# Router logits computed with the router's weights stationary, turned by VectorE and placed by DMAs

## The chip, the cores and the metric

The kernel runs on one core of a Trainium2 chip. The metric is the device time of one execution in microseconds (us); a lower number is better. The engines of the core are named PE (TensorE's matmuls), PEld (TensorE's weight loads), DVE (VectorE), ACT (ScalarE), POOL (GpSimd) and SP (SyncE, which issues all of this kernel's DMAs; its queue is written SPq).

## The reference, cut to what matters

A batch of 8 images is cut into patches and embedded, joined with text tokens (548 tokens of 192 features per image), passed through one attention layer, and then through a mixture of experts. The change lies in the mixture of experts, and there in the first two lines only:

```python
logits = jnp.einsum('td,ed->te', xt, router_w)      # 4384 tokens, 192 features, 16 experts
probs = jax.nn.softmax(logits, axis=-1)
topk_w, topk_idx = jax.lax.top_k(probs, 8)
topk_w = topk_w / jnp.sum(topk_w, axis=-1, keepdims=True)
comb = zeros((T, 16)).at[arange(T)[:, None], topk_idx].add(topk_w)
for e in range(16):                                  # 8 experts of width 128, 8 of width 256
    h = gelu(xt @ w1[:, off:off + wd])
    out = out + comb[:, e:e + 1] * (h @ w2[off:off + wd, :])
```

## The kernel before

The first part of the program (until about 240 us) is the attention of the eight images. From there on the mixture of experts runs, over nine token tiles: t = 0 to 7 with 512 tokens each, t = 8 with 288. Each token tile takes 24 steps, k = 0 to 23, one for each 128 rows of the experts' hidden width. Tokens are columns: `x2` holds the normalised tokens with features on the partitions, and one step is a chain over four engines:

- `up` on PE: five matmuls into a PSUM bank (three banks in turn), 128 hidden rows by 512 tokens
- `gelu` on ACT (L884): PSUM to `act`
- `weigh` on DVE (L1303): `act` times `gate`, the expert's weights of all tokens, spread over the partitions
- `act_round` on ACT (L674, tile `act_hi`), then `act_rest` on DVE (L1035, tile `act_lo`): the two parts of `act` that fp32r matmuls read
- `down` on PE: five matmuls that read `act_hi` and `act_lo` and add into the output's banks

PE runs ahead of itself: in its program `up(j + 3)` stands before `down(j)`, with j counting the steps of all tiles. DVE's loop runs, for each j, `weigh(j + 1)`, `act_rest(j)` and then the side work of step k (function `beside`); ACT's runs `gelu(j + 1)`, `act_round(j)`, side work. All `act` tiles exist three times, so `gelu(j)` waits for `act_rest(j - 3)` and `act_round(j)` for `down(j - 3)`.

The side work prepares the next tile, t + 1, while tile t runs. For the router of tiles 2 to 8 it is, before the change:

- PE, after `down` of step 11: `logits(t + 1)`. The tokens' columns are the weights, 128 at a time, and the router's 32 columns move (16 experts, with the rounded and the remaining part of their weights side by side). Four groups of 128 tokens times three matmuls make twelve; three groups of 96 make nine for t + 1 = 8. The result has tokens on partitions, in PSUM bank 3.
- DVE, step 13: `router_shift` (L1187 to L1191, tiles `lsum`, `lmax`, `lsub`) adds the two parts and takes off the maximum.
- ACT, step 13: `logits_exp` (L815, tile `lexp`). Exp and gelu need different tables, so a table load stands before it and another before the next gelu.
- DVE, steps 14 to 17: `router_top`, `router_left`, `router_weights` (tile `comb`) and `turn_comb` (L1227, tile `ct_t`), which turns the weights in 32x32 blocks.
- SP: `store_ct` (L371) writes `ct_t` to `comb_dram`, four DMAs that put the blocks in place; `gates` (L458) spreads one expert's row over the partitions of one of four `gate` buffers, one DMA per expert.

SP's program has a fixed order. In tile t, behind the gates of experts 10 to 13, it holds `store_out(t - 1)` (six DMAs, L463), `load_res(t + 2)` (L424), `load_rb(t)` (six DMAs, L405), the gates of experts 14 and 15 and `store_ct(t + 1)`. Expert 14 is first weighed in step 20, expert 15 in step 22, and expert 0 of the next tile in the `weigh` that stands in step 23.

Of the kernel before, what the change touches and what calls it, by code (L numbers as in the profile page):

```python
# [32 lines left out]
P = 128  # L33
# [23 lines left out]
E = 16  # L57
# [28 lines left out]
def width(t):  # L86
    return WIDTHS[t]


def segs(t):  # L90

    return SEG if width(t) % (SEG * BLOCK) == 0 else SEG - 1
# [7 lines left out]
def ct_after(t):  # L100

    return 16 * sum(ct_dmas(u) for u in range(t + 1))
# [53 lines left out]
def early_fusion(nc, first_patches, patches, txt, tok_w, tok_b, gammas, gn_w, gn_b, attn_w, w1, w2, out):  # L156
# [3 lines left out]
    def sb(name, shape, dt=F32, scope=ctx):  # L160
        return scope.enter_context(nc.sbuf_tensor(name, shape, dt))

    def sem(name):
        return ctx.enter_context(nc.semaphore(name))

    with ctx:
# [67 lines left out]
        ot = [ot0, ot1]  # L234
        out_t = sb("out_t", [HD, TW])
        ct_t = sb("ct_t", [P, SEG * BLOCK])

        aw_hi, aw_lo = sb("aw_hi", [P, 2, AW], F32R), sb("aw_lo", [P, 2, AW], F32R)
        rw = sb("rw", [P, 2, 2, E], F32R)
# [64 lines left out]
        down_done, sums_read, out_ready = sem("down_done"), sem("sums_read"), sem("out_ready")  # L304
        out_stored, ld_rb = [sem(f"out_stored{i}") for i in range(2)], [sem(f"ld_rb{i}") for i in range(2)]
        xn2_turned, x2_stored, ld_x2, ct_turned = sem("xn2_turned"), sem("x2_stored"), [sem("ld_x2_0"), sem("ld_x2_1")], sem("ct_turned")
        h_stored, ld_res = sem("h_stored"), [sem(f"ld_res{i}") for i in range(3)]

        block = ctx.enter_context(nc.Block())
# [18 lines left out]
        def _(sp):  # L328
# [44 lines left out]
            def x2_rows(t):  # L373
                return x2_dram[0:D * width(t)].rearrange("(d n) -> d n", d=D)
# [10 lines left out]
            def load_x2(t):  # L385

                n = width(t)
                sp.wait_ge(x2_stored, 16 * sum(width(u) // segs(u) // BLOCK for u in range(BY_BLOCKS, t + 1)))
                sp.dma_start(x2_raw[:, 0, 0:n], x2_rows(t)[0:P, :]).then_inc(ld_x2[0], 16)
                for p0 in (0, HD):  # L390
                    sp.dma_start(x2_raw[p0:p0 + HD, 1, 0:n], x2_rows(t)[P:D, :]).then_inc(ld_x2[1], 16)

            def block_views(rows_, t):

# [53 lines left out]
            def gates(t, first, end):  # L448
                n = width(t)
                for e in range(first, end):  # L450

                    last = LAST_OF[(e - 4) % E] + 1
                    if e >= 4:
                        sp.wait_ge(gated, nth(t, NW, last))
                    elif t:
                        sp.wait_ge(gated, nth(t - 1, NW, last))
                    src = comb_dram[e, FROM[t]:FROM[t] + n].partition_broadcast(P)
                    sp.dma_start(gate[e % 4][:, 0:n], src).then_inc(ld_gate[e % 4], 16)  # L458

            def store_out(t):  # L460
                sp.wait_ge(out_ready, t + 1)
                for dst, src in block_views(out_rows, t):
                    sp.dma_start(dst, src).then_inc(out_stored[t % 2], 16)  # L463
# [22 lines left out]
            for t in range(1, NTT):  # L486
                nxt = t + 1 < NTT
                sp.wait_ge(ct_stored, ct_after(t))
                gates(t, 0, 8)
                if nxt:  # L490
                    store_x2(t + 1)
                gates(t, 8, 10)
                if nxt:
                    load_x2(t + 1)
                gates(t, 10, 14)
                store_out(t - 1)
                if t + 2 < NTT:
                    load_res(t + 2)
                load_rb(t)
                gates(t, 14, 16)  # L500
                if nxt:
                    store_ct(t + 1)
# [167 lines left out]
        def _(sc_eng):  # L670
# [250 lines left out]
            def beside(t, k):  # L921

                if t + 1 == NTT:
                    return
                if k == 0:
                    second_norm(t + 1, 0)
                elif k == 1:
                    second_norm(t + 1, 1)
                elif k == 9:
                    x2_round(t + 1, 0)  # L930
                elif k == 10:
                    x2_round(t + 1, 1)
                elif k == 13:
                    logits_exp(t + 1)

            gelu(0)
# [11 lines left out]
        def _(dve):  # L948
# [230 lines left out]
            def wide(ap):  # L1179
                return ap.unsqueeze(2).broadcast_to([ap.shape[0], ap.shape[1], E])  # L1180

            def router_shift(t, bank=U_BANK):
                n = segs(t)
                r = width(t) // n
                dve.wait_ge(lg_done, t + 1)
                parts = ps[:r, bank, 0:n * 2 * E].rearrange("p (g i e) -> p g e i", g=n, i=2)
                dve.tensor_reduce(lsum[:r, 0:n, :], parts, AX.X, ALU.add)  # L1187
                dve.drain()
                dve.tensor_reduce(lmax[:r, 0:n], lsum[:r, 0:n, :], AX.X, ALU.max)
                dve.drain()  # L1190
                dve.tensor_tensor(lsub[:r, 0:n, :], lsum[:r, 0:n, :], wide(lmax[:r, 0:n]), ALU.subtract).then_inc(l_sub, 1)  # L1191
# [175 lines left out]
            def beside(t, k):  # L1367

                if k in (4, 5, 6):
                    turn_out(t - 1, (k - 4,))  # L1370
                elif k in (7, 8):
                    add_out(t - 1, (k - 7,))
                elif k == 11:
                    add_out(t - 1, (2,))
                if 20 <= k < 23 and t + 2 < NTT:
                    second_part(t + 2, k - 20)
                if t + 1 == NTT:
                    return
                if k in (2, 3):
                    turn_x2(t + 1, k - 2)  # L1380
                elif k == 9:
                    x2_rest(t + 1, 0)
                elif k == 10:
                    x2_rest(t + 1, 1)
                elif k == 13:
                    router_shift(t + 1)
                elif k == 14:
                    router_top(t + 1)
                elif k == 15:
                    router_left(t + 1)  # L1390
                elif k == 16:
                    router_weights(t + 1)
                elif k == 17:
                    turn_comb(t + 1)

            weigh(0)
# [13 lines left out]
        def _(pe):  # L1410
# [200 lines left out]
            def logits(t, bank=U_BANK):  # L1611
                n = segs(t)
                r = width(t) // n
                pe.wait_ge(x2_lo, nth(t, 2, 2))
                if t == 0:
                    pe.wait_ge(rw_ready, 1)
                elif t == BY_BLOCKS:
                    pe.wait_ge(ct_copied, BY_BLOCKS)
                for g in range(n):
                    c = slice(g * r, (g + 1) * r)  # L1620
                    x = [x2[t % 2][:, i, c] for i in range(3)]
                    near, rest = [rw[:, i, :, :].rearrange("p i e -> p (i e)") for i in range(2)]
                    last = series(ps[:r, bank, 2 * E * g:2 * E * (g + 1)], [(x[0], near), (x[1], near), (x[2], rest)])
                last.then_inc(lg_done, 1)

# [211 lines left out]
```

## Time and profile before

| | us |
|---|---|
| median of three runs | 765.95 (765.46 to 766.73) |
| the profiled execution | 763.07 |
| its span, first to last instruction | 761.3 |
| PE busy in the span | 719.3 (94%) |
| DVE busy | 582.1 (76%) |
| ACT busy | 467.0 (61%) |
| POOL busy | 153.0 (20%) |
| mean granted clock of TensorE | 0.994 |

The profile is that of one execution. A start time is counted from the beginning of the span. A row that ends in "x12" groups twelve instructions that follow each other; its duration is that of the whole group. Matmuls overlap, so a matmul of 0.39 us may be followed by the next after 0.23 us: what a matmul costs is the distance between starts. The bracket at a row's end is the time the engine was idle before it and what it waited for.

### The profile page before, as it was taken

The numbers are of one execution on the slowest core, as the hardware profiler recorded it, in microseconds if no ns is written. First come the engines' busy times: TensorE is split into PE (matmuls) and PEld (weight loads), VectorE is DVE, ScalarE is ACT, GpSimd is POOL, SyncE is SP. The second block draws the span as 40 slices with busy tenths as digits, with TensorE's granted clock in tenths as the row PEclk, the third lists the DMA queues.
The fourth block names the chain that finished last, engine by engine and source line by source line (L and its number), as shares of the span: only waits on it lengthen the run. The fifth ranks groups of instructions, "written<-read, shape, count | busy, mean of one in ns | idle before, by whom it ended". The sixth has DMA issues, their size and how long they took to land.

```text
span 761.3 us, 13137 instructions
## 1 busy us (share of the span) xinstructions
PE 719.3 (94%) x4265; PEld 605.2 (79%) x4265; DVE 582.1 (76%) x1616; ACT 467.0 (61%) x1041; POOL 153.0 (20%) x254
## 2 busy tenths in 40 slices
PE   5988999999998799999999999999999999999996
PEld 4777878888986577788888888888888888888895
DVE  7888988998888686677777777767777777677675
ACT  3677778778777646456456456456456456456453
POOL 3062654753543870000000000000000000000000
PEclk9999999999999999999999999999999999999998
DMA  6700011011022651455256255255265255244242
GB/s 196 210 23 22 1 45 44 13 34 44 30 79 65 166 163 45 97 136 128 74 132 128 76 134 125 77 131 132 72 128 136 74 133 121 73 132 94 46 87 43
DMA packets 120564, 70.13 MB, mean 92 GB/s; under 512 B 82000, under 2 KB 100496, under 8 KB 120496
## 3 DMA queue, kind: packets, MB, share of 16 engines
q1 hardware_dynamic: 120496, 69.31, 36.6%
q8 instruction: 33, 0.54, 0.3%
q14 instruction: 35, 0.29, 0.1%
HBM read 58.65 MB, written 10.63 MB: 91 GB/s over the span
## 4 chain that ended last, share of the span: by engine, by line
PE 66%; DVE 21%; ACT 4%; issue 3%; DVEq 3%; DMA 2%; SPq 1%; POOL 0%; POOLq 0%
PE ps L1412 65%; DVE sc L1072 4%; DVE pr L1094 4%; ACT pr L754 2%; DVE nm L1079 2%; DVE k_lo L1035 1%; DVE st L989 1%; DVE gst L1100 1%; DVEq L1077 1%; DVE h L1138 1%; DMA pat<-patches 1%; ACT xa_hi L674 1%; DVE act L1303 1%; DMA gate<-comb_dram 1%; DVE q_lo L1035 1%
## 5 line engine op out<-in xcount | busy, mean ns | idle before, releaser
L884 ACT ACTIVATE act<-ps 128x512 f32<-128x512 f32 (+1 forms) x216 | 124.7, 578 | 205.4 <-PE ps L1412 205.3
L1303 DVE TENSOR_TENSOR act<-act,gate 128x512 f32<-128x512 f32 (+1 forms) x216 | 145.5, 673 | 126.5 <-ACT act L884 117.1
L1412 PE MATMUL ps<-x,w_hi 128*128 128x512 f32 (+1 forms) x648 | 215.2, 387 | 2.2 <-ACT act L884 2.2
L1412 PE MATMUL ps<-x,w_lo 128*128 128x512 f32 (+1 forms) x432 | 165.4, 383 | 0.0
L1035 DVE TENSOR_TENSOR act_lo<-act,act_hi 128x512 fp32r<-128x512 f32 (+1 forms) x216 | 146.1, 676 | 0.2
L1412 PEld LDWEIGHTS ps<-x,w_hi 128*128 128x128 f32 x648 | 120.5, 188 | 27.1 <-ACT act L884 2.7
L674 ACT ACTIVATE act_hi<-act 128x512 fp32r<-128x512 f32 (+1 forms) x216 | 130.2, 603 | 3.2 <-DVE act L1303 3.1
L1412 PEld LDWEIGHTS ps<-x,w_lo 128*128 128x128 f32 x432 | 81.3, 188 | 16.5
L1412 PE MATMUL ps<-act_hi,w_hi 128*128 128x512 f32 (+1 forms) x216 | 83.2, 385 | 3.3 <-DVE act_lo L1035 3.3
L535 POOL TENSOR_TENSOR rstdb<-vepsb,neg_half 128x4 f32<-128x4 f32 x9 | 9.1, 1010 | 379.8 <-DVE vepsb L1168 379.8
L1412 PE MATMUL ps<-act_lo,w_hi 128*128 128x512 f32 (+1 forms) x216 | 83.2, 385 | 0.0
L1412 PE MATMUL ps<-act_hi,w_lo 128*128 128x512 f32 (+1 forms) x216 | 83.2, 385 | 0.0
L1412 PE MATMUL ps<-act_lo,w_r 128*128 128x512 f32 (+1 forms) x216 | 82.4, 381 | 0.0
L1412 PE MATMUL ps<-act_hi,w_r 128*128 128x512 f32 (+1 forms) x216 | 81.4, 377 | 0.0
L754 ACT ACTIVATE pr<-sc,nm 128x580 f32<-128x580 f32 (+4 forms) x120 | 66.3, 555 | 13.2 <-DVE nm L1079 13.2
L1561 PE MATMUL ps<-ident,pr 128*128 128x128 f32 (+1 forms) x360 | 45.3, 277 | 15.0 <-DVE q_lo L1035 6.7
L674 ACT ACTIVATE pt<-ps 128x384 f32<-128x384 f32 (+3 forms) x120 | 46.4, 470 | 17.0 <-PE ps L1561 16.8
L1561 PEld LDWEIGHTS ps<-ident,pr 128*128 128x128 f32 (+1 forms) x360 | 39.1, 133 | 20.1 <-issue 7.4
L1412 PEld LDWEIGHTS ps<-act_hi,w_hi 128*128 128x128 f32 x216 | 40.5, 188 | 14.8 <-DVE act_lo L1035 5.6
L1072 DVE CUSTOM_DVE_ANT_0 sc<-ps,decay 128x548 f32<-128x548 f32 (+4 forms) x120 | 49.4, 453 | 1.6 <-PE ps L1412 1.5
L1412 PEld LDWEIGHTS ps<-act_hi,w_r 128*128 128x128 f32 x216 | 40.6, 188 | 9.0
L1412 PEld LDWEIGHTS ps<-act_lo,w_r 128*128 128x128 f32 x216 | 40.4, 187 | 9.0
(183 smaller groups left out, 1200.3 us busy)
## 6 DMA issues: line engine op xcount, KB each, us to landing
gate<-comb_dram SPq DMA_DIRECT2D x128, 256.0 KB, 3.6
w_raw<-w SPq DMA_DIRECT2D x16, 384.0 KB, 3.7
h_dram<-h SPq DMA_DIRECT2D x8, 384.0 KB
res<-h_dram SPq DMA_DIRECT2D x8, 384.0 KB, 3.9
rb<-h_dram SPq DMA_DIRECT2D x48, 64.0 KB, 2.5
out<-rb SPq DMA_DIRECT2D x48, 64.0 KB, 1.9
x_dram<-xn_t SPq DMA_DIRECT2D x24, 96.0 KB, 2.4
gate<-comb_dram SPq DMA_DIRECT2D x16, 144.0 KB, 3.2
```

The source lines that it names most:

```text
L535: pool.tensor_tensor(rs[:, :], ve[:, :], neg_half[:, 0:n], ALU.pow)
L674: return a.activation(dst, src, ACT.Copy)
L754: last = a.activation(pr[s][:r, cols], sc[s][:r, cols], ACT.Exp, bias=nm[s][:r, I:I + 1], accum_out=row_sum[s][:r, I:I + 1])
L884: a.activation(act[j % 3][:, 0:n], ps[:, up_bank(j), 0:n], ACT.Gelu_apprx_tanh).then_inc(gelu_done, 1)
L989: dve.bn_stats(s6[:rows(I), I, :], tokens(h, b, I))
L1035: return dve.tensor_tensor(dst, src, hi, ALU.subtract)
L1072: dve.tensor_tensor_reduce(out=sc[s][:r, OFF[I]:OFF[I] + n], in0=psf[:r, at:at + n], in1=decay[:r, hh, 0:n], scale=1.0 / 8, scalar=0.0 if ...
L1079: dve.tensor_scalar(nm[s][:, cols], mx[s][:, cols], -1.0, None, ALU.mult).then_inc(nm_ready, 1)
L1094: last = dve.tensor_scalar(t, t, inv_den[s][:rows(I), I:I + 1], None, ALU.mult)
L1303: dve.tensor_tensor(act[j % 3][:, 0:n], act[j % 3][:, 0:n], gate[e % 4][:, 0:n], ALU.mult).then_inc(gated, 1)
L1412: return pe.matmul(dst, w, x, start=start, stop=stop)
L1561: return pe.transpose(ps[:n, bank, at:at + P], pr[s][:, src:src + n], ident[:, :])
```

## The change

For the tiles 2 to 8 the matmul is swapped: the router's 32 columns are the weights, and all tokens of the tile move, three matmuls of 512 columns (288 for tile 8) in place of twelve (nine). The result now has the 32 router columns on partitions and tokens along the row. DVE's `turn_logits`, in step 12, turns it in 32x32 blocks from PSUM into `lg_t`; SP's `place_logits`, four DMAs (three for tile 8) of 32 x 4 x 32 elements, puts the blocks in place in `lg`, with tokens on partitions as before; `router_shift` reads `lg` and waits for these DMAs. `router_shift` and `logits_exp` stand in step 14 in place of 13, and the DVE steps behind them are each one later, `turn_comb` in 18. Tiles 0 and 1 are as before.

```diff
--- before.py
+++ after.py
@@ -234,6 +234,7 @@
         ot = [ot0, ot1]
         out_t = sb("out_t", [HD, TW])
         ct_t = sb("ct_t", [P, SEG * BLOCK])
+        lg_t, lg = sb("lg_t", [BLOCK, TW]), sb("lg", [P, SEG, BLOCK])
 
         aw_hi, aw_lo = sb("aw_hi", [P, 2, AW], F32R), sb("aw_lo", [P, 2, AW], F32R)
         rw = sb("rw", [P, 2, 2, E], F32R)
@@ -304,6 +305,7 @@
         down_done, sums_read, out_ready = sem("down_done"), sem("sums_read"), sem("out_ready")
         out_stored, ld_rb = [sem(f"out_stored{i}") for i in range(2)], [sem(f"ld_rb{i}") for i in range(2)]
         xn2_turned, x2_stored, ld_x2, ct_turned = sem("xn2_turned"), sem("x2_stored"), [sem("ld_x2_0"), sem("ld_x2_1")], sem("ct_turned")
+        lg_turned, lg_placed = sem("lg_turned"), sem("lg_placed")
         h_stored, ld_res = sem("h_stored"), [sem(f"ld_res{i}") for i in range(3)]
 
         block = ctx.enter_context(nc.Block())
@@ -389,6 +391,14 @@
                 sp.dma_start(x2_raw[:, 0, 0:n], x2_rows(t)[0:P, :]).then_inc(ld_x2[0], 16)
                 for p0 in (0, HD):
                     sp.dma_start(x2_raw[p0:p0 + HD, 1, 0:n], x2_rows(t)[P:D, :]).then_inc(ld_x2[1], 16)
+
+            def place_logits(t):
+
+                sp.wait_ge(lg_turned, t - BY_BLOCKS + 1)
+                n = width(t) // segs(t) // BLOCK
+                for i in range(n):
+                    src = lg_t[:, 0:width(t)].rearrange("c (g i e) -> c i g e", g=segs(t), e=BLOCK)[:, i, :, :]
+                    sp.dma_start(lg[i * BLOCK:(i + 1) * BLOCK, 0:segs(t), :], src).then_inc(lg_placed, 16)
 
             def block_views(rows_, t):
 
@@ -493,6 +503,8 @@
                 if nxt:
                     load_x2(t + 1)
                 gates(t, 10, 14)
+                if nxt:
+                    place_logits(t + 1)
                 store_out(t - 1)
                 if t + 2 < NTT:
                     load_res(t + 2)
@@ -930,7 +942,7 @@
                     x2_round(t + 1, 0)
                 elif k == 10:
                     x2_round(t + 1, 1)
-                elif k == 13:
+                elif k == 14:
                     logits_exp(t + 1)
 
             gelu(0)
@@ -1179,11 +1191,19 @@
             def wide(ap):
                 return ap.unsqueeze(2).broadcast_to([ap.shape[0], ap.shape[1], E])
 
+            def turn_logits(t):
+                dve.wait_ge(lg_done, t + 1)
+                dve.transpose(lg_t[:, 0:width(t)], ps[0:BLOCK, U_BANK, 0:width(t)]).then_inc(lg_turned, 1)
+
             def router_shift(t, bank=U_BANK):
                 n = segs(t)
                 r = width(t) // n
-                dve.wait_ge(lg_done, t + 1)
-                parts = ps[:r, bank, 0:n * 2 * E].rearrange("p (g i e) -> p g e i", g=n, i=2)
+                if t < BY_BLOCKS:
+                    dve.wait_ge(lg_done, t + 1)
+                    parts = ps[:r, bank, 0:n * 2 * E].rearrange("p (g i e) -> p g e i", g=n, i=2)
+                else:
+                    dve.wait_ge(lg_placed, ct_after(t) - ct_after(BY_BLOCKS - 1))
+                    parts = lg[:r, 0:n, :].rearrange("p g (i e) -> p g e i", i=2)
                 dve.tensor_reduce(lsum[:r, 0:n, :], parts, AX.X, ALU.add)
                 dve.drain()
                 dve.tensor_reduce(lmax[:r, 0:n], lsum[:r, 0:n, :], AX.X, ALU.max)
@@ -1382,15 +1402,17 @@
                     x2_rest(t + 1, 0)
                 elif k == 10:
                     x2_rest(t + 1, 1)
-                elif k == 13:
+                elif k == 12:
+                    turn_logits(t + 1)
+                elif k == 14:
                     router_shift(t + 1)
-                elif k == 14:
+                elif k == 15:
                     router_top(t + 1)
-                elif k == 15:
+                elif k == 16:
                     router_left(t + 1)
-                elif k == 16:
+                elif k == 17:
                     router_weights(t + 1)
-                elif k == 17:
+                elif k == 18:
                     turn_comb(t + 1)
 
             weigh(0)
@@ -1616,10 +1638,14 @@
                     pe.wait_ge(rw_ready, 1)
                 elif t == BY_BLOCKS:
                     pe.wait_ge(ct_copied, BY_BLOCKS)
+                near, rest = [rw[:, i, :, :].rearrange("p i e -> p (i e)") for i in range(2)]
+                if t >= BY_BLOCKS:
+                    x = [x2[t % 2][:, i, 0:width(t)] for i in range(3)]
+                    series(ps[0:2 * E, bank, 0:width(t)], [(near, x[0]), (near, x[1]), (rest, x[2])]).then_inc(lg_done, 1)
+                    return
                 for g in range(n):
                     c = slice(g * r, (g + 1) * r)
                     x = [x2[t % 2][:, i, c] for i in range(3)]
-                    near, rest = [rw[:, i, :, :].rearrange("p i e -> p (i e)") for i in range(2)]
                     last = series(ps[:r, bank, 2 * E * g:2 * E * (g + 1)], [(x[0], near), (x[1], near), (x[2], rest)])
                 last.then_inc(lg_done, 1)
 
```

PE, at the end of step 11 of tile 2: `act_hi2` and `act_lo2` belong to `down` of step 11, `rw` is the router's weights, `x2_1` the tokens of tile 3; the row with `act_hi0` opens `down` of step 12. Before:

```order
L1412 MATMUL ps<-act_lo2,w2_r 128x512
L1412 MATMUL ps<-rw,x2_1 128x32 [waits x2_lo]
L1412 MATMUL ps<-rw,x2_1 128x32 x11
L1412 MATMUL ps<-x2_0,w1_hi 128x512 [waits gelu_done]
L1412 MATMUL ps<-x2_0,w1_lo 128x512
L1412 MATMUL ps<-x2_0,w1_hi 128x512 x2
L1412 MATMUL ps<-x2_0,w1_lo 128x512
L1412 MATMUL ps<-act_hi0,w2_hi 128x512 [waits act_lo_ready]
```

The same place after:

```order
L1434 MATMUL ps<-act_lo2,w2_r 128x512
L1434 MATMUL ps<-x2_1,rw 32x512 [waits x2_lo]
L1434 MATMUL ps<-x2_1,rw 32x512 x2
L1434 MATMUL ps<-x2_0,w1_hi 128x512 [waits gelu_done]
L1434 MATMUL ps<-x2_0,w1_lo 128x512
L1434 MATMUL ps<-x2_0,w1_hi 128x512 x2
L1434 MATMUL ps<-x2_0,w1_lo 128x512
L1434 MATMUL ps<-act_hi0,w2_hi 128x512 [waits act_lo_ready]
```

Twelve narrow matmuls became three wide ones at the same place.

DVE, steps 12 to 15 of a middle tile: `act0` to `act2` are the three buffers of `act`, and the row with `gate3` and `act2` is `weigh` of step 14. Before:

```order
L1035 TENSOR_TENSOR act_lo0<-act0,act_hi0 128x512 [waits act_hi_ready]
L1303 TENSOR_TENSOR act2<-act2,gate3 128x512 [waits ld_gate3,gelu_done]
L1035 TENSOR_TENSOR act_lo1<-act1,act_hi1 128x512 [waits act_hi_ready]
L1187 TENSOR_REDUCE lsum<-ps 128x64 [waits lg_done]
L1189 TENSOR_REDUCE lmax<-lsum 128x4
L1191 TENSOR_TENSOR lsub<-lsum,lmax 128x64
L1303 TENSOR_TENSOR act0<-act0,gate3 128x512 [waits ld_gate3,gelu_done]
L1035 TENSOR_TENSOR act_lo2<-act2,act_hi2 128x512 [waits act_hi_ready]
L1200 MAX top<-lexp 128x8 [waits l_exp]
```

The same place after:

```order
L1047 TENSOR_TENSOR act_lo0<-act0,act_hi0 128x512 [waits act_hi_ready]
L1196 STREAM_TRANSPOSE lg_t<-ps 32x512 [waits lg_done]
L1323 TENSOR_TENSOR act2<-act2,gate3 128x512 [waits ld_gate3,gelu_done]
L1047 TENSOR_TENSOR act_lo1<-act1,act_hi1 128x512 [waits act_hi_ready]
L1323 TENSOR_TENSOR act0<-act0,gate3 128x512 [waits ld_gate3,gelu_done]
L1047 TENSOR_TENSOR act_lo2<-act2,act_hi2 128x512 [waits act_hi_ready]
L1207 TENSOR_REDUCE lsum<-lg 128x64 [waits lg_placed]
L1209 TENSOR_REDUCE lmax<-lsum 128x4
L1211 TENSOR_TENSOR lsub<-lsum,lmax 128x64
L1323 TENSOR_TENSOR act1<-act1,gate0 128x512 [waits ld_gate0,gelu_done]
L1047 TENSOR_TENSOR act_lo0<-act0,act_hi0 128x512 [waits act_hi_ready]
L1220 MAX top<-lexp 128x8 [waits l_exp]
```

The wait for PE's logits stands one step earlier, and the shift is one step later behind a wait for the DMAs.

SP, behind the last gates of the first fourteen experts: `lg` is the placed logits, `rb0` the output rows, `res0` and `rb1` loads for later. After the change:

```order
L468 DMA gate1<-comb_dram 128x512 [waits gated]
L401 DMA lg<-lg_t 32x4x32 [waits lg_turned]
L401 DMA lg<-lg_t 32x4x32 x3
L473 DMA out<-rb0 32x16x32 [waits out_ready]
L473 DMA out<-rb0 32x16x32 x5
L434 DMA res0<-h_dram 128x4x192 [waits ln2_normed]
L415 DMA rb1<-h_dram 32x16x32 x6
L468 DMA gate2<-comb_dram 128x512 [waits gated]
L468 DMA gate3<-comb_dram 128x512 [waits gated]
L373 DMA comb_dram<-ct_t 16x4x32 [waits ct_turned]
```

The two rows on `lg` are new; before, the store of `out` followed directly on the gate.

## Rows read from the trace of the kernel before

**Rows 1.** Window 411.5 to 468.5 us (one token tile): busy us and instructions by engine, clock.

```profile
411.50:468.50 57.00, 57.00 (x254) 46.38 (x253) 41.53 (x91) 32.40 (x58) 1.79 (x3) 1.00 0.48 112
```

**Rows 2.** All waits of PE from 290 us to the end: total, times, longest.

```profile
PE ps L1412 <- DVE act_lo L1035: 1.1, 1, 1.1
```

**Rows 3.** Timeline of PE around the logits of tile 3: start, duration, instruction.

```profile
411.37 0.39 PE L1412 MATMUL ps<-act_lo,w_r 128*128 128x512 f32 x1
411.60 1.41 PE L1412 MATMUL ps<-rw,x 128*128 128x32 f32 x12
412.85 0.48 PE L1412 MATMUL ps<-x,w_hi 128*128 128x512 f32 x1
...
414.11 0.39 PE L1412 MATMUL ps<-act_hi,w_hi 128*128 128x512 f32 x1
...
418.75 0.39 PE L1412 MATMUL ps<-act_hi,w_hi 128*128 128x512 f32 x1
...
421.06 0.39 PE L1412 MATMUL ps<-act_hi,w_hi 128*128 128x512 f32 x1
```

**Rows 4.** Timeline of PE around the logits of tile 8 (288 tokens).

```profile
696.70 0.86 PE L1412 MATMUL ps<-rw,x 128*96 128x32 f32 x9
...
697.73 0.39 PE L1412 MATMUL ps<-x,w_lo 128*128 128x512 f32 x1
```

**Rows 5.** Timeline of DVE over the same stretch as rows 3.

```profile
411.27 0.69 DVE L1303 TENSOR_TENSOR act<-act,gate 128x512 f32<-128x512 f32 x1 [1.02 <-ACT act L884]
411.88 0.69 DVE L1035 TENSOR_TENSOR act_lo<-act,act_hi 128x512 fp32r<-128x512 f32 x1
413.04 0.29 DVE L1187 TENSOR_REDUCE lsum<-ps 128x64 f32<-128x128 f32 x1 [0.47 <-PE ps L1412]
...
416.16 0.69 DVE L1303 TENSOR_TENSOR act<-act,gate 128x512 f32<-128x512 f32 x1 [2.23 <-ACT act L884]
416.76 0.69 DVE L1035 TENSOR_TENSOR act_lo<-act,act_hi 128x512 fp32r<-128x512 f32 x1
```

**Rows 6.** Transposes on DVE from PSUM: duration min/median/max in ns.

```profile
L1320 DVE STREAM_TRANSPOSE out_t<-ps x9: 485/718/719, 339.3 to 754.9; 64x512 f32<-64x512 f32 x8, 64x288 f32<-64x288 f32 x1
```

**Rows 7.** Timeline of SP's queue over the same stretch.

```profile
408.74 3.03 SPq L463 DMA_DIRECT2D out<-rb  x6
...
415.88 1.33 SPq L458 DMA_DIRECT2D gate<-comb_dram  x2
423.62 1.73 SPq L371 DMA_DIRECT2D comb_dram<-ct_t  x4
```

**Rows 8.** DMAs issued from 395 to 456 us: KB each, median us to landing.

```profile
out<-rb SPq DMA_DIRECT2D x6, 64.0 KB, 1.9
...
rb<-h_dram SPq DMA_DIRECT2D x6, 64.0 KB, 2.7
x_dram<-xn_t SPq DMA_DIRECT2D x4, 96.0 KB, 2.4
...
comb_dram<-ct_t SPq DMA_DIRECT2D x4, 8.0 KB, 1.5
```

**Rows 9.** Timeline of ACT over the same stretch.

```profile
413.96 0.26 ACT L815 ACTIVATE lexp<-lsub 128x64 f32<-128x64 f32 x1 [0.90 <-DVE lsub L1191]
414.23 1.28 ACT L884 ACT_TABLE_LOAD   x1
415.53 0.60 ACT L884 ACTIVATE act<-ps 128x512 f32<-128x512 f32 x1
```

**Rows 10.** Timeline in tile 0: PE waits for a late `act_lo`.

```profile
284.85 0.69 DVE L1035 TENSOR_TENSOR act_lo<-act,act_hi 128x512 fp32r<-128x512 f32 x1
...
285.59 0.50 PE L1412 MATMUL ps<-act_hi,w_hi 128*128 128x512 f32 x1 [0.28 <-DVE act_lo L1035]
```

**Rows 11.** Gate loads issued at 415.8 to 416.3 us, landing.

```profile
gate<-comb_dram SPq DMA_DIRECT2D x1, 256.0 KB, 3.8
```

**Rows 12.** Gate loads issued at 509.9 to 510.5 us, behind the loads of `x_raw`.

```profile
gate<-comb_dram SPq DMA_DIRECT2D x1, 256.0 KB, 7.0
```

## The prediction

> **What bounds the kernel now.** I began with the busy time by stage, since the change touches only the router of tiles 2 to 8. In one token tile of the mixture of experts PE is busy for 57.00 of 57.00 us at full granted clock, DVE for 41.5 and ACT for 32.4 [rows 1]. Then the waits: from 290 us on PE waits once, for 1.1 us [rows 2]. So PE's instruction stream is the time of this stage. What leaves PE's stream is won in full, until one of PE's inputs is late; what goes onto DVE or a DMA costs nothing, until it makes `act_lo` late for `down`. Last I read the timelines of PE, DVE, ACT and SP around one set of logits. Ahead lie 6 tiles with 512 tokens (2 to 7) and one with 288 (8).
>
> **What PE saves.** `down` opens every (421.06 - 414.11) / 3 = 2.317 us, ten matmuls, so 0.232 us each [rows 3]. From the first logits matmul to the next `down` are 2.51 us, of which five matmuls of `up` are 1.16: the twelve cost 1.35 us [rows 3]. The new three move 512 columns each, as `up` and `down` do, so 3 x 0.232 = 0.70. Saved: 0.65 per tile. Tile 8: 697.73 - 696.70 - 0.23 = 0.80 for nine [rows 4]; three with 288 columns are 3 x 0.232 x 288/512 = 0.39 (an estimate by columns); saved 0.41. Sum: 6 x 0.65 + 0.41 = 4.3 us. That is the most the change can give, since nothing else leaves PE.
>
> **The wait in step 12.** DVE's `turn_logits` now waits for the logits one step earlier. In the times of tile 2: PE starts the third matmul at 411.60 + 0.46 = 412.06 and, with 0.39 us for it [rows 3], is done at 412.45. DVE starts at 412.48. A turn of 512 columns from PSUM takes 0.72 us [rows 6], on fewer partitions no less, so I take 0.71: done at 413.19. Behind it on DVE are `weigh` of step 14, which ran at 411.27 and now ends at 413.9, and `act_lo` of step 13, which ran at 411.88 [rows 5] and now ends at 414.5. `down` of step 13 opens at 414.11 - 0.65 + 2.32 = 415.78 [rows 3]. The delay of nearly 2 us and the extra 0.71 us of DVE are hidden by that lead: cost 0. ACT's next `act_round` gets its input at 413.9, about when the gelu before it is over.
>
> **The wait in step 14.** SP's queue is free (its last gate of that part goes out before the store at 408.74), so it issues at 413.2. The nearest DMA in form is the store of `ct_t`: four in 1.73 us, 0.43 apart [rows 7]. The fourth goes out at 414.5 and lands L later, so `router_shift` starts at 414.55 + L. DVE is through with the two steps ahead of it by 415.8. From there the old rows give the distances. Exp on ACT starts 413.96 - 413.04 = 0.92 after the shift's first instruction [rows 5, 9]. Behind exp come a table load of 1.28 and the gelu [rows 9], then `weigh`, `act_round` and `act_lo`, which ends at 416.76 + 0.69 = 417.45, 3.49 after exp began [rows 5]. Before, that `act_lo` was for `down` of step 14, opening at 418.75: 1.30 us of slack [rows 3]. After, it is for `down` of step 15, whose turn would come at 421.06 - 0.65 = 420.41. It is ready at 414.55 + L + 0.92 + 3.49 = 418.96 + L. A PE that waits restarts 0.05 us after `act_lo` ends, and its first matmul lasts 0.50 instead of 0.39, the weight load being no longer hidden [rows 10]: 0.16 together. So the stall is S = 418.96 + L + 0.16 - 420.41 = L - 1.3, if positive. One tile gains 0.65 - S = 1.95 - L.
>
> **L decides, and no row shows it.** No DMA in this trace goes from SBUF to SBUF. This one has 128 runs of 128 bytes, the store of `ct_t` 64 and lands in 1.5; the stores of `rb` have 512 and land in 1.9, those of `xn_t` 768 in 2.4 [rows 8]. Between the first two by runs: 1.5 + 0.4 x 64/448 = 1.56. A load from DRAM takes 2.7 with 512 runs [rows 8]; that one has to read DRAM, which this one need not, so 2.7 is the far end. The near end is 1.3, where S is zero; below that nothing more is won. I take 1.55, by the store of the same shape.
>
> The Trainium skill ("DMA: Bandwidth & Descriptors", the two cost components) gives a DMA a fixed cost of about 2.0 us, most of it the receipt of the write at the target. By that, L would be 2.0 and the gain gone. The stores of `ct_t` with 1.5 us speak against it here [rows 8]; whether an SBUF target does the same no row shows.
>
> **Sum.** S = 0.25, so 0.40 per tile: 6 x 0.40 = 2.4. Tile 8 has one DMA fewer (0.43) and a turn shorter by 0.23 [rows 6], against a slot that moves only 0.41 ahead in place of 0.65: its `act_lo` is on time and its 0.41 stay. Together 2.8 us. The profiled execution took 763.07 (a span of 761.3 and 1.8 around it) and would take 760.3; the median of the runs is 2.9 above that execution, so 765.95 - 2.8 = 763.2.
>
> **What SP pushes back.** The four DMAs hold the queue from 413.2 to 415.0. The store of `out`, the loads of `res` and `rb`, which took 415.88 - 408.74 = 7.14 us [rows 7], move from 408.74 to 415.0, and the gate of expert 14 from 415.88 to 422.1. It lands 3.8 later [rows 11], at 425.9. Its `weigh` in step 20 stands six steps behind that of step 14: 411.27 + 6 x 2.317 + 1.35 = 426.5 before, 426.1 after. Just in time; and late by up to 2.3 us would still cost nothing, since in a plain step `act_lo` ends about 2.5 us ahead of its `down` (412.57 against 416.43, less the 1.35 of logits [rows 3, 5]) and PE wants it some 0.2 early. `store_ct` moves with `turn_comb`: a step of 2.3 less the 0.4 saved, plus the 1.3 by which DVE's chain has come closer to PE, 3.1 us, from 423.62 to 426.7 [rows 7]. The first gate of the next tile then lands near 433.4, for a `weigh` at 435.4. Cost 0, with 2 us left. `load_res` and `load_rb` are used a good step or a whole tile later.
>
> **Rivals.**
> - No stall (L at 1.3 or less, or the chain behind exp a little shorter): the full 4.3 us, 761.7. For it: writes into SBUF may be acknowledged sooner than the stores to DRAM. Against it: twice the runs of `ct_t`. 0.22.
> - The stall eats the gain (L between 1.76 and 2.2). At L = 2.0: 6 x -0.05 + 0.41 = 0.1 us, 765.9. For it: the stores of `rb` at 1.9 and `xn_t` at 2.4 [rows 8]. This is where the skill's 2.0 leads. 0.25.
> - Slower by the same wait: each tile loses from L = 1.95, the whole from 2.02, by over 0.2% from 2.27. With the 2.7 of `rb` [rows 8]: 6 x 0.75 - 0.41 = 4.1 us more, 770.0. Against it: its source is DRAM. 0.08.
> - The gate of expert 14 is late. With 7.0 us to landing [rows 12] it comes at 429.1, 3.0 behind its `weigh`; 2.3 are covered, 0.7 stall PE in each of seven tiles: 4.9 - 2.8 = 2.1 us slower, 768.0. Against it: the 7.0 came behind the large loads of `x_raw`, while rows 11 stand behind the same store and loads that are ahead of it here. 0.05.
> - The forecast (L from 1.4 to 1.75): 763.2 ± 1. 0.40.
>
> **The numbers.** A measurement of this kernel can tell some 0.2%, 1.5 us, from no change. Faster by more than that needs L under 1.76: 0.22 + 0.40 = 0.62. Within it: 0.25. Slower: 0.08 + 0.05 = 0.13. The range goes from 761.2 (the full saving, with half a us of scatter) to 767.0, over the flat case; it leaves out the slower ones.
>
> **What the profile after would show.** The logits as three matmuls 0.23 apart, with the next `up` 0.70 behind their start; if they take as long as twelve, the saving was never there. The turn near 0.71 us behind a DVE wait of some 2 us. The DMAs 0.43 apart with about 1.55 to landing: this is the number that would make me wrong. `lsum` waiting for the DMA for some 0.3 us. In PE's waits, six for `act_lo` of 0.1 to 0.4 us, at `down` of step 15, none for tile 8. Gate waits in step 20 of at most a few tenths that nobody passes on. If PE waits at another step, or for longer, my chain behind exp is wrong.

## The result: slower by 0.84%

| | before | changed |
|---|---|---|
| median of the runs | 765.71 (4 runs, 765.43 to 766.73) | 772.38 (4 runs, 772.01 to 773.22) |
| the profiled execution | 763.07 | 772.01 |
| its span | 761.3 | 770.2 |

The ratio is 1.0084, with a 95% interval of 1.0069 to 1.0098: 5.3 to 7.5 us slower. Forecast were 2.8 us faster, with a range up to 767.0.

From 345 us to the end PE waited nowhere before; the one wait of [rows 2] is at 292.0 us, in tile 0. After, this is the whole list (engine and tile that waited, what for; total, times, longest):

```profile
PE ps L1434 <- DVE act_lo L1047: 7.4, 8, 1.3
```

One of them falls in each of the tiles 1 to 7 (while the next tile's router is prepared), the eighth near the end of tile 8. PE around the logits of tile 3, which answers to [rows 3] (the changed kernel is here 4.17 us later on the time axis):

```profile
415.77 0.86 PE L1434 MATMUL ps<-x,rw 128*32 128x512 f32 x3
416.47 0.39 PE L1434 MATMUL ps<-x,w_hi 128*128 128x512 f32 x1
...
417.64 0.40 PE L1434 MATMUL ps<-act_hi,w_hi 128*128 128x512 f32 x1
...
424.37 0.39 PE L1434 MATMUL ps<-x,w_lo 128*128 128x512 f32 x1
425.78 0.50 PE L1434 MATMUL ps<-act_hi,w_hi 128*128 128x512 f32 x1 [1.02 <-DVE act_lo L1047]
```

The three matmuls cost 0.70 us, as forecast. The `down` of step 15 should open at 424.37 + 0.23 = 424.60; it opens at 425.78, and its unhidden weight load costs 0.11 more. DVE in the same stretch [rows 5]:

```profile
416.67 0.70 DVE L1196 STREAM_TRANSPOSE lg_t<-ps 32x512 f32<-32x512 f32 x1 [2.25 <-PE ps L1434]
417.31 0.64 DVE L1323 TENSOR_TENSOR act<-act,gate 128x512 f32<-128x512 f32 x1
417.88 0.67 DVE L1047 TENSOR_TENSOR act_lo<-act,act_hi 128x512 fp32r<-128x512 f32 x1
418.48 0.69 DVE L1323 TENSOR_TENSOR act<-act,gate 128x512 f32<-128x512 f32 x1
419.08 0.69 DVE L1047 TENSOR_TENSOR act_lo<-act,act_hi 128x512 fp32r<-128x512 f32 x1
421.26 0.29 DVE L1207 TENSOR_REDUCE lsum<-lg 128x64 f32<-128x128 f32 x1 [1.50 <-DMA lg<-lg_t]
...
424.43 0.69 DVE L1323 TENSOR_TENSOR act<-act,gate 128x512 f32<-128x512 f32 x1 [2.29 <-ACT act L896]
425.04 0.69 DVE L1047 TENSOR_TENSOR act_lo<-act,act_hi 128x512 fp32r<-128x512 f32 x1
```

And SP's queue [rows 7], first merged, then its fourth placing DMA alone:

```profile
417.40 2.61 SPq L401 DMA_DIRECT2D lg<-lg_t  x4
420.05 3.31 SPq L473 DMA_DIRECT2D out<-rb  x6
```

```profile
419.41 0.60 SPq L401 DMA_DIRECT2D lg<-lg_t  x1
```

That fourth DMA with its KB and its us from issue to landing:

```profile
lg<-lg_t SPq DMA_DIRECT2D x1, 16.0 KB, 1.8
```

ACT [rows 9]:

```profile
422.18 0.26 ACT L827 ACTIVATE lexp<-lsub 128x64 f32<-128x64 f32 x1 [1.92 <-DVE lsub L1211]
422.51 1.28 ACT L896 ACT_TABLE_LOAD   x1
423.80 0.60 ACT L896 ACTIVATE act<-ps 128x512 f32<-128x512 f32 x1
```

Read from the bottom: `act_lo` ends at 425.73, 3.55 after exp began (3.49 forecast); exp begins 0.92 after the shift (0.92); the shift begins 3.86 after SP's first issue (2.90 forecast). Nearly the whole surprise is in that last distance. The fourth DMA goes out 2.01 us after the first, 0.67 from start to start and not 0.43, and it lands 1.83 after its issue, not 1.55.

**Where the time went.** PE does the same 216 `down`s in both kernels, so the starts of `down` can be laid side by side, and the difference of two executions grows exactly where one loses. I use this for every kernel below, from step 10 of tile 1 to the last `down` ("the changed part"). In us against the kernel before:

| | ahead | six tiles, each | tile 8's router | end of tile 8 | changed part |
|---|---|---|---|---|---|
| changed kernel | +3.5 | +0.60 to +0.66 | +1.22 | +0.42 | +5.4 |

"Ahead" is the stretch from the start to step 10 of tile 1. A tile is -0.64 in step 11 and +1.26 in steps 14 and 15. Tile 8's router is -0.40 and +1.62. The 3.5 us ahead lie where both kernels do the same work. They are no part of the result: the same measure over the kernels below gives from 0.7 to 5.6 for that stretch. The profiled execution of the kernel before lies 2.6 us under the median of its runs. Two rows of it and of the changed one, from 250 us, with the granted clock behind the busy times, show one difference in that stretch; that it is the whole of it is not shown. Before:

```profile
250.00:260.00 10.00, 8.06 (x40) 5.90 (x42) 5.47 (x6) 5.08 (x12) 9.28 (x14) 0.83 0.70 195
260.00:270.00 10.00, 9.04 (x44) 6.70 (x41) 7.82 (x15) 7.21 (x13) 8.41 (x12) 1.00 0.67 192
```

After:

```profile
250.00:260.00 10.00, 6.82 (x26) 5.07 (x27) 5.05 (x7) 4.83 (x11) 8.56 (x14) 0.75 0.69 183
260.00:270.00 10.00, 9.84 (x49) 7.18 (x49) 6.12 (x11) 5.64 (x11) 9.29 (x13) 0.91 0.58 174
```

### The profile page after: what moved, and what is told of

It is laid out like the page before. It is cut to its first block, busy times and chain, and to the rows that moved or that the text cites. A ratio compares the mean times of both kernels' runs of the same rounds, so it can differ in the third digit from the quotient of the medians.

```text
span 770.2 us, 13051 instructions
## 1 busy us (share of the span) xinstructions
PE 718.9 (93%) x4205; PEld 599.1 (78%) x4205; DVE 583.6 (76%) x1623; ACT 467.2 (61%) x1041; POOL 151.5 (20%) x254
## 4 chain that ended last, share of the span: by engine, by line
PE 56%; DVE 23%; issue 5%; ACT 5%; DMA 4%; SPq 3%; DVEq 3%; POOL 0%; ACTq 0%; POOLq 0%
PE ps L1434 55%; DVE sc L1084 4%; DVE pr L1106 4%; ACT pr L766 2%; DMA lg<-lg_t 2%; DVE nm L1091 2%; SPq L401 2%; DVE act_lo L1047 1%; DVE act L1323 1%; DVE k_lo L1047 1%; DMA gate<-comb_dram 1%; DVEq L1089 1%; DVE gst L1112 1%; DVE st L1001 1%; DVE h L1150 1%
## 5 line engine op out<-in xcount | busy, mean ns | idle before, releaser
L1047 DVE TENSOR_TENSOR act_lo<-act,act_hi 128x512 fp32r<-128x512 f32 (+1 forms) x216 | 144.4, 669 | 0.2
L1434 PEld LDWEIGHTS ps<-act_hi,w_hi 128*128 128x128 f32 x216 | 40.5, 188 | 26.4 <-DVE act_lo L1047 17.6
```

What stands on the lines that cost most here:

```text
L1047: return dve.tensor_tensor(dst, src, hi, ALU.subtract)
L1434: return pe.matmul(dst, w, x, start=start, stop=stop)
```

## The experiments

The theory after the result: but for 0.4 us at the end of tile 8, all that is lost is the wait for the placing DMAs, handed on through exp and gelu to `down` of step 15. The rivals were the two new tiles in SBUF, DVE's longer wait in step 12, and the step in which exp stands.

**layout**: the two tiles alone, in the kernel before.

```diff
+        lg_t, lg = sb("lg_t", [BLOCK, TW]), sb("lg", [P, SEG, BLOCK])
```

> The kernel before with the two new tiles lg_t and lg allocated and never used. Theory (the placing is what costs): by the starts of down, the changed kernel loses 5.4 us from step 11 of tile 1 on (six tiles at 0.63, tile 8 at 1.22, 0.42 at the end of tile 8), while 3.5 us of the difference of the two profiled executions lie ahead of that, where both kernels do the same; that part is scatter of single executions, so this kernel takes 765.7 within 0.5 us. Rival (the new tiles move others in SBUF and that costs something in the attention part): the timed difference is 6.7 and not 5.4, so 1.3 us or more are from the layout and this kernel takes 767 to 769.

Measured: ratio 1.0008 (0.9995 to 1.0021), 12 runs against 29. The changed part +0.01 us. The new tiles cost nothing. The 29 runs of the kernel before lie between 762.9 and 768.4, a scatter as wide as that of the stretch ahead.

**no_place**: neither the DMAs nor the wait for them.

```diff
-                if nxt:
-                    place_logits(t + 1)
-                    dve.wait_ge(lg_placed, ct_after(t) - ct_after(BY_BLOCKS - 1))
```

> The changed kernel without the DMAs that place the logits and without the wait for them; router_shift, still in step 14, reads a tile of zeros, so the router's result is not computed from the logits. Theory: the matmul swap gains 0.64 us in each of six tiles and 0.41 in tile 8, DVE's wait for the logits in step 12 stays (15 us in all) and costs nothing, and PE's wait in step 15 is gone: 765.7 - 4.3 = 761.4, with PE waits for act_lo after 340 us near 0. Rival (DVE's longer wait in step 12 together with the turn is what starves PE): most of the 7.4 us of PE waits stay, 768 or more.

Measured: ratio 0.9969 (0.9957 to 0.9982), 763.70 against 766.30. The changed part is -3.9: -0.63 in each of six tiles, -0.40, and +0.30 at the end of tile 8. No wait of PE for `act_lo` from 340 us on is long enough to be listed (0.15 us). The medians differ by 2.6 us and not by 3.9; the profiled execution spent 4.2 us more than the kernel before's in the stretch ahead, and no run separates the rest. DVE's waits from 340 us on:

```profile
DVE act L1321 <- ACT act L894: 84.3, 128, 2.3
DVE lg_t L1195 <- PE ps L1432: 15.4, 7, 2.3
DVE act L1321 <- DMA gate<-comb_dram: 3.0, 3, 1.4
```

DVE still stands 15.4 us before the turn, and it costs nothing. The rival of step 12 is out.

**moved_only**: the kernel before, with only the steps moved.

```diff
-                elif k == 13:
+                elif k == 14:
                     router_shift(t + 1)
```

(and in the same way exp, and the DVE steps behind, up to `turn_comb` in 18)

> The kernel before (twelve narrow matmuls, no turn, no DMAs) with router_shift, exp and the DVE steps behind them one step later, as the change has them. Theory: the step's place costs nothing by itself; the logits are in PSUM before act_lo of step 14 ends, exp starts about one step (2.3 us) less the old wait later against a down one step later, and PE waits nowhere after 340 us: each step from down to down is as in the kernel before, to 0.05 us. Rival (putting exp behind act_round of step 14 is what starves PE): down of step 15 opens 1 us or more late in each of seven tiles.

Measured in one execution: the changed part 0.00, no tile differs by more than 0.01. The place of exp is free as long as its input is there.

**twice**: every placing DMA twice.

```diff
+                for i in range(n):
+                    sp.dma_start(lg_2[i * BLOCK:(i + 1) * BLOCK, 0:segs(t), :], src).then_inc(lg_placed, 16)
```

> The changed kernel with each placing DMA issued twice, the second time into a spare tile, and router_shift waiting for all of them. Theory (the time of the DMAs goes straight into PE's stall): four more issues of 0.65 us make the placed logits 2.6 us later, so down of step 15 opens 1.26 + 2.6 = 3.9 us late in each of six tiles, three more at 0.65 in tile 8 give 1.6 + 2.0 = 3.6; over the changed kernel 6 x 2.6 + 2.0 = 17.6 us, 790 in all by the median of 772.4. Rival (the stall is from something else of step 14 or 15, or the DMAs of one tile run side by side): less than 5 us over the changed kernel.

Measured: ratio 1.0432 (1.0415 to 1.0449), 798.83. That is 26 us over the changed kernel, where 17.6 were expected. In step 14 the six tiles lose 3.7 where the changed kernel lost 1.15: 2.55 more, and four more issues at 0.64 are 2.57. But then steps 15 (and once 16) add 1.4 to 2.9, where the changed kernel had 0.1. Tile 8 loses 1.1 more than in the changed kernel, not 2.0. PE in tile 2:

```profile
427.85 0.39 PE L1438 MATMUL ps<-x,w_lo 128*128 128x512 f32 x1
431.83 0.79 PE L1438 MATMUL ps<-act_hi,w_hi 128*128 128x512 f32 x1 [3.59 <-DVE act_lo L1051]
432.42 0.63 PE L1438 MATMUL ps<-act_hi,w_lo 128*128 128x512 f32 x1
432.85 0.63 PE L1438 MATMUL ps<-act_lo,w_hi 128*128 128x512 f32 x1
...
435.72 0.39 PE L1438 MATMUL ps<-act_hi,w_hi 128*128 128x512 f32 x1
```

```profile
431.80:435.30 3.50, 3.47 (x9) 2.75 (x10) 3.41 (x17) 1.29 (x3) 0.00 (x0) 0.54 0.96 185
```

Matmuls stand 0.43 apart instead of 0.23, and the mean granted clock of these 3.5 us is 0.54: the lower level, 1.2 GHz, for nearly all of them, right after PE stood still for 3.6 us. The clock fell at the end of each of the six waits of 3.5 to 3.6 us (at most 0.7 us before PE went on), and not at tile 8's of 2.5 us. So the time of the DMAs goes into the stall one for one, and the longer stall has a price of its own.

**What makes the DMAs slow.** A run is a piece of 128 bytes that lies together in memory; the change's DMA has 128 of them, `ct_t`'s store 64. Two kernels, each executed once, have one property of `ct_t`'s store each [rows 7, 8]. **half**: 16 of the 32 partitions, so 64 runs.

```diff
-                    src = lg_t[:, 0:width(t)]...
-                    sp.dma_start(lg[i * BLOCK:(i + 1) * BLOCK, 0:segs(t), :], src)
+                    src = lg_t[0:E, 0:width(t)]...
+                    sp.dma_start(lg[i * BLOCK:i * BLOCK + E, 0:segs(t), :], src)
```

> The changed kernel with the placing DMAs over 16 of the 32 partitions: 64 runs of 128 bytes each, as the store of ct_t has; the other rows of the placed tile stay zero, so half of each block's tokens get no logits. Question: is it the number of runs or the target in SBUF that makes an issue 0.65 us and the landing 1.8, where ct_t's store has 0.43 and 1.5? If the runs: 0.43 and 1.5 here, the last lands 0.65 + 0.3 = 1.0 us earlier, and down of step 15 opens 0.3 us late in place of 1.26. If the target: 0.65 and 1.8 stay and so does the stall.

Measured: 0.67 between issues, 1.8 to land, 1.20 of stall per tile. The number of runs hardly matters. **to_dram**: the same blocks to DRAM.

```diff
-                    sp.dma_start(lg[i * BLOCK:(i + 1) * BLOCK, 0:segs(t), :], src)
+                    sp.dma_start(lg_dram[i * BLOCK:(i + 1) * BLOCK, 0:segs(t), :], src)
```

> The changed kernel with the placing DMAs writing the same blocks to DRAM in place of the SBUF tile, which stays zero, so the router's result is not computed from the logits; the wait for them stays. Same question from the other side. If the target in SBUF makes them slow: 0.43 to 0.5 to issue and 1.5 to 1.6 to land, and down of step 15 opens 0.1 to 0.5 us late. If the 128 runs do: 0.65 and 1.8, stall 1.26 as in the changed kernel.

Measured: 0.64 between issues and 1.9 to land for the tiles of 512, with 1.20 of stall; but 0.42 and 1.5 for tile 8, with no stall at all (-0.40). That this last one is on time agrees with the working of the stall: with the DMA times that I had assumed, tile 8 does what was forecast. SP's queue in tiles 3 and 8 of that kernel:

```profile
414.45 2.52 SPq L402 DMA_DIRECT2D lg_dram<-lg_t  x4
...
701.85 1.26 SPq L402 DMA_DIRECT2D lg_dram<-lg_t  x3
```

**padded**: the target's runs kept apart.

```diff
+        lg = sb("lg", [P, SEG, 2 * BLOCK])        # blocks in [:, :, 0:BLOCK]
```

> The changed kernel with the rows of the placed tile spread: each group of 32 logits is followed by 32 unused elements, so the four runs of 128 bytes of one partition no longer join to one of 512 at the target. Question still open: half (64 runs into SBUF: 0.65 us to issue, 1.8 to land) spoke against the number of runs, to_dram (0.60 and 1.9 for 512 tokens, where the target joins up, but 0.42 and 1.4 for tile 8, where it does not) against SBUF as the target. Theory: what costs is a target whose runs join while the source's do not; then issues 0.43 apart and 1.5 to landing, the last one 1.0 us earlier, down of step 15 opens 0.3 us late in six tiles and on time in tile 8: 4 x less stall, some 6.5 us under the changed kernel, about 766. Rival (any DMA within SBUF costs 0.65 and 1.8): as the changed kernel, 772.

Measured: ratio 1.0082 (1.0061 to 1.0103), 0.67 and 1.8 as in the changed kernel. The theory of the joined target is out.

**forms**: another form of the DMA in each tile, the logits in step 10.

```diff
+                    dst, src = {2: (lg_2[p, g, :], own), 3: (lg_2[p, g, :], row), 4: (lg_dram[p, g, 0:BLOCK], row),
+                                5: (lg_dram[p16, g, 0:BLOCK], row16), 6: (lg_2[p16, g, :], row16),
+                                7: (lg_dram[p16, g, 0:BLOCK], own16), 8: (lg_dram[p, g, 0:BLOCK], own)}[t]
```

> The kernel with the logits in step 10 (there the placing is hidden), in which the placing DMAs of each tile have another form and write to a spare tile or to DRAM; router_shift reads zeros, so the router's result is not computed from the logits. Tile 2: as in the change (32 partitions, four runs of 128 bytes that lie apart in the source, to SBUF). 3: source one run of 512 bytes, to SBUF. 4: that source, to DRAM rows whose groups lie apart. 5: as 4 with 16 partitions, which is the form of ct_t's store (0.43 to issue, 1.5 to land). 6: as 5, to SBUF. 7: 16 partitions, source runs apart, to DRAM. 8: 32 partitions, source runs apart, to DRAM, three groups. Theory A (the number of source partitions, 32 or 16, sets the issue time): 0.65 in 2, 3, 4, 8 and 0.43 in 5, 6, 7. Theory B (source runs that lie apart): 0.65 in 2, 7, 8 and 0.43 in 3 to 6. Theory C (SBUF as the target): 0.65 in 2, 3, 6 and 0.43 in the others; the DMAs of to_dram, 0.60 in tiles 2 to 7, speak against it unless their joined target is a second cause. Landings of 1.8 and 1.5 go with them.

Measured: SP's queue, one row for each of the tiles 2 to 8.

```profile
359.05 2.62 SPq L411 DMA_DIRECT2D lg<-lg_t  x4
...
415.44 2.48 SPq L411 DMA_DIRECT2D lg<-lg_t  x4
...
471.82 2.52 SPq L411 DMA_DIRECT2D lg_dram<-lg_t  x4
...
528.21 2.50 SPq L411 DMA_DIRECT2D lg_dram<-lg_t  x4
...
584.60 2.48 SPq L411 DMA_DIRECT2D lg<-lg_t  x4
...
640.99 2.91 SPq L411 DMA_DIRECT2D lg_dram<-lg_t  x4
...
697.14 1.26 SPq L411 DMA_DIRECT2D lg_dram<-lg_t  x3
```

All but the last are 0.62 or more apart; only three groups to DRAM have 0.42 and 1.5 to landing. The slow ones land in 1.75 to 1.9, but for two of tile 7 (2.4 and 2.2), whose group also has one distance of 1.04; they belong with tile 8's late DMA below. Theories A, B and C all fail: the form of tile 5 (16 partitions, one source run, to DRAM) takes 0.64, and `ct_t`'s store with the same numbers 0.43. Why is open. What is known is that neither the number of runs, nor whether they lie together in the source, nor SBUF as the target alone decides. Two differences were never varied: the strides of the target in DRAM, and that `ct_t`'s four blocks lie on four groups of partitions while all four DMAs out of `lg_t` read the same ones. The second can't decide alone either, since tile 8's three to DRAM read the same partitions and are fast.

**shift15**: the wait hidden from behind, one more step for the DMAs.

```diff
-                elif k == 14:
+                elif k == 15:
                     router_shift(t + 1)
```

(exp in 15, the steps behind up to `turn_comb` in 19)

> The changed kernel with router_shift, exp and all DVE steps behind them one step later (shift and exp in 15, turn_comb in 19). Theory: in tile 2 the placed logits were there at 421.2; act_lo of step 15 is over near 422.1, so the shift starts at once and exp some 0.8 us later than now, against a down that is a step of 2.32 later: the stall of 1.26 becomes a slack of 0.2, and the kernel takes 761.4 to 762.2 (0.4 if gates at the end of tile 8 come late). Rival (the chain shift, exp, table load, gelu costs PE wherever the placing ends): the stall stays near 1.3 per tile and the kernel takes 771 to 773. Second rival: gates of the next tile come late because store_ct moves another 2.3 us: DVE waits for gates grow from 4 to over 15 us and the gain is lost, 765 or more.

Measured: ratio 0.9962 (0.9946 to 0.9977), 763.44 against 766.30; the changed part -3.7, with 0.44 lost at the end of tile 8. The stalls of step 15 are gone. DVE's waits for gates do grow to 20.0 us, as the second rival said, but DVE's lead hides them; PE's one wait, 0.2 us, is at the end of tile 8.

**logits10**: the wait hidden from ahead, the logits one step earlier.

```diff
-                if k == 11 and t + 1 < NTT:
+                if k == 10 and t + 1 < NTT:
                     logits(t + 1)
```

> The changed kernel with PE's logits after down of step 10 in place of 11, all else as changed. Theory: the turn starts at the end of act_lo of step 12, 2.25 us earlier against the rest, so the placed logits are there before act_lo of step 14 is over; PE's waits in step 15 go and the gain of 4.3 stays: 761.4 to 762. Rival (x2 of the next tile is not ready for PE in step 10): PE waits for x2_lo once per tile and the time is 765 or more.

Measured: ratio 0.9947 (0.9928 to 0.9967), 762.39 against 766.30; the changed part -3.6, of which 0.63 are lost at the end of tile 8. DVE no longer waits before the turn at all. **padded10** combines it with padded:

```diff
-                if k == 11 and t + 1 < NTT:
+                if k == 10 and t + 1 < NTT:
+        lg = sb("lg", [P, SEG, 2 * BLOCK])        # blocks in [:, :, 0:BLOCK]
```

> padded together with the logits in step 10. Both theories: there the placing is hidden anyway, so it gains at most a few tenths over logits10: 762 to 763.

Measured: 762.18 against 766.23, ratio 0.9947 (0.9929 to 0.9964), the same.

**gates_first**: logits10, and in tile 8 the last two gates ahead of `load_rb`.

```diff
-                load_rb(t)
+                if nxt:
+                    load_rb(t)
                 gates(t, 14, 16)
+                if not nxt:
+                    load_rb(t)
```

> The kernel with the logits in step 10, and in tile 8 the gates of experts 14 and 15 ahead of load_rb(8) in SP's queue. Theory: in tile 8 the six loads of rb took 4.2 us to issue in place of 3.0, and the gate of expert 14 behind them came 2.1 us late, which cost PE 0.63 us in logits10; ahead of them it is on time: PE waits for act_lo after 340 us 0, the changed part 4.9 us shorter than in the kernel before, and the time 4.5 to 5 us under it, 761.3. Rival (the gate is late for another reason, such as its own landing): 0.5 us of PE waits stay.

SP's queue near the end, logits10 first, then gates_first:

```profile
739.91 4.24 SPq L415 DMA_DIRECT2D rb<-h_dram  x6
744.20 0.93 SPq L468 DMA_DIRECT2D gate<-comb_dram  x2
```

```profile
739.85 0.98 SPq L468 DMA_DIRECT2D gate<-comb_dram  x2
740.88 2.92 SPq L415 DMA_DIRECT2D rb<-h_dram  x6
```

Measured: 761.56 against 766.23, ratio 0.9945 (0.9927 to 0.9962). PE waits nowhere from 340 us on; the changed part is -4.2 (not the -4.9 that was expected), that is 6 x -0.63 and -0.40: the full saving of the swap. Its median is the lowest here, but the runs don't separate it from logits10 and padded10 (the three ratios are 0.9945 to 0.9947).

## Why the prediction was wrong

- **What PE saves.** Right: 0.64 per tile and 0.40 for tile 8 in every kernel with the swap, 0.65 and 0.41 forecast.
- **The wait in step 12.** Right: DVE waits 2.25 us (near 2 forecast) and a turn takes 0.70; no_place shows that it costs nothing.
- **The wait in step 14.** The chain was right (exp 0.92 behind the shift, `act_lo` 3.49 against 3.55 behind exp, restart and unhidden load as worked out), and so was the place of the stall. The failed step is the one that put the fourth DMA out "at 414.5" and let it land L later. Two terms of it were mis-sized. The spacing between issues was taken as certain, 0.43 by the store of `ct_t`; it is 0.67, and enters three times: 0.7 us. L was taken as 1.55 and is 1.83: 0.3. Together the stall is 1.26 in place of 0.25, and 6 x 1.0 turns the forecast's 6 x -0.40 into the measured 6 x +0.6. With 1.6 for tile 8 and 0.4 at its end, which the forecast had at nothing, the forecast's -2.8 becomes the +5.4 of the changed part.
- **The bounds.** In the tiles of 512 L stayed within its bounds, but no bound was put on the spacing, which multiplies by three. The store of `out`, six in 3.03 us [rows 7], showed that a spacing of 0.50 was possible. Both terms right would still have missed: with 0.67 and 1.83 the sum is 6 x 0.6 - 0.41 = +3.2, so 769.1. The rest is tile 8 and the stretch ahead. In the rivals' terms it went the way of "slower by the same wait": its turning point, L = 2.02, is well passed by 1.83 plus the 0.7 of the spacings. That rival had the sign and the place right and was given 0.08.
- **Tile 8.** Forecast on time, measured +1.62 of stall. Its third placing DMA, issued at 706.45, landed 3.2 us later instead of 1.8, and DVE went on at 709.63: some 1.3 of the 1.6 us. Padded showed 3.5 at the same place, to_dram 1.5. The trace has a companion for it: a transfer of 16 KB that the profile calls "instruction", on a queue that is not SP's. In the changed kernel it begins at 707.47 and lasts 1.05 us; in the DMA queues of 707.4 to 707.5 us it is this line:

```profile
q8 instruction: 1, 0.02, 43.4%
```

Of the 297 placing DMAs in the profiled executions of the ten kernels that have them, 15 took over 2.1 us to land, and each of the 15 was under way together with such a transfer; the others took 1.9 at most. Eight of those met one too, but only in their first 0.3 us or from 1.3 us after their issue on. In to_dram the transfer begins at 704.03, when tile 8's last placing DMA (issued at 702.69) is 0.15 us from landing. No run moved these transfers, so that they cause the delay is likely, not shown.
- **What SP pushes back.** Right for tiles 2 to 7: PE never waited in step 20. The gate at the end of tile 8 was not in the list. It was late before too, by 0.9 us that DVE's lead hid; in no_place, which pushes nothing back in SP's queue, it already costs 0.30. It stands behind the six loads of `rb`, which took 3.0 us to issue before and 3.9 to 4.2 in no_place, the changed kernel and logits10; there one of the six took 1.3 to 1.7 us, and such an "instruction" transfer began within 0.1 us of it. In gates_first the gates go out ahead of the loads and the cost is gone; but in its execution no such transfer met the loads (2.92 us), so how much of the 0.6 the new order bought is open. (The terms given for `store_ct` add up to 3.2, not 3.1; nothing hangs on it.)

The Trainium skill's fixed 2.0 us for a DMA ("DMA: Bandwidth & Descriptors", "Anatomy of one DMA", the two cost components) was nearer to the landing measured, 1.8 to 1.9, than the 1.55 read from the neighbouring row. The page fits it to DMAs that GpSimd issues, which the prediction left out; here SP issues them. Taken alone, with a spacing of 0.43, it would still have said no change.

## What to carry to other kernels

Before a chain of small DMAs is put in front of a wait, price it as (n - 1) spacings plus a landing and bound both: the spacing counts n - 1 times, and a row of a DMA that looks alike does not fix it. A producer that saves TensorE time but hands its result to a slower path should start a step earlier or be read a step later; here one line (`k == 10`) turned +0.8% into -0.5%. To find what a change costs, lay the starts of one repeated instruction of the bounding engine side by side: it separates 0.1 us per tile from 5 us of scatter elsewhere.

## What was not expected of the hardware

- Nearly identical small DMAs differ by half in issue time: 0.43 us and 1.5 to landing for `ct_t`'s store, 0.62 to 0.72 and 1.75 to 1.9 for nine forms out of `lg_t` (the change's own, five of forms, half, padded, to_dram), 0.42 and 1.5 for three groups of 32 to DRAM. Unexplained.
- The profile's "instruction" transfers of 16 KB came together with every placing DMA that landed late (2.1 to 3.7 us in place of 1.75 to 1.9). Their places shift from kernel to kernel, so a wait with no slack can be hit in one version and spared in the next.
- After a stall of 3.6 us the granted clock was 0.54 over the next 3.5 us (twice), and the tile lost another 1.5 us; in the six tiles this was 1.3 to 1.5, once 2.8. The changed kernel's stalls, at most 1.35 us long, left the clock at 1.00; the row of 415.7 to 473.4 us, with one stall of 1.0:

```profile
415.70:473.40 57.70, 56.68 (x245) 45.31 (x243) 41.92 (x91) 32.38 (x58) 1.79 (x3) 1.00 0.47 112
```
